# Final stage of a two-layer kernel: ScalarE normalizes seven of the eight pairs in one operation, VectorE multiplies by gamma and adds x in wide ones, GpSimd makes the biases

## What is computed

```
def _layer_norm(r, gamma, beta):
    mu = jnp.mean(r, axis=-1, keepdims=True)
    var = jnp.mean(jnp.square(r - mu), axis=-1, keepdims=True)
    return (r - mu) * jax.lax.rsqrt(var + LN_EPS) * gamma + beta
...
x = x + _layer_norm(z + out, gamma, beta)      # z = _layernorm(x)
```

## Time and profile before

| what | us |
|---|---|
| median of three runs | 1231.94 |
| profiled execution, its own time | 1231.25 |
| its span, first to last instruction | 1229.4 |
| last scatter into `dOUT` landed, first load of r issued | 1191.87 |
| last instruction of VectorE ends | 1224.96 |

### The profile page before, as it was taken

How to read it: one execution, slowest core, us unless ns; L and a number is a source line. 1 busy time by engine, 2 the same in 40 slices (tenths; PEclk the granted TensorE clock), 3 DMA queues, 4 the chain that set the end, 5 groups by cost and what they waited for, 6 DMA issues and landing times.

```text
span 1229.4 us, 24074 instructions
## 1 busy us (share of the span) xinstructions
PE 1095.7 (89%) x8282; PEld 1011.8 (82%) x8282; DVE 911.8 (74%) x1992; ACT 784.1 (64%) x1617; POOL 641.2 (52%) x573
## 2 busy tenths in 40 slices
PE   3678999988988999999999887999999999999950
PEld 2577887877876888888898777999999999999950
DVE  5787887686665666666657886899878778877868
ACT  4766666654234556555656666887778778877835
POOL 2444443442344556655644667886665544454435
PEclk8779999999899999999999988999999999999985
DMA  6644441231226579667746956556689766666539
GB/s 207 220 158 157 143 142 69 97 116 61 66 94 203 139 197 270 150 161 198 201 87 163 300 176 185 130 152 169 161 191 225 175 189 191 191 168 176 165 80 215
DMA packets 141864, 201.07 MB, mean 164 GB/s; under 512 B 28992, under 2 KB 115792, under 8 KB 134704
## 3 DMA queue, kind: packets, MB, share of 16 engines
q1 hardware_dynamic: 108880, 158.89, 39.0%
q0 software_dynamic: 32320, 40.13, 19.0%
q10 hardware_dynamic: 544, 0.52, 0.1%
HBM read 153.16 MB, written 46.48 MB: 162 GB/s over the span
## 4 chain that ended last, share of the span: by engine, by line
PE 70%; DVE 15%; DMA 4%; ACT 4%; issue 3%; POOL 2%; SPq 0%; DVEq 0%; ACTq 0%; POOLq 0%
PE pb L2198 16%; PE quad L2179 14%; PE quad L1230 13%; PE pb L1245 7%; PE pb L354 4%; PE quad L300 4%; PE pb L368 2%; DVE Dm L529 2%; PE quad L2173 2%; PE quad L2151 1%; PE pb L265 1%; PE pb L1214 1%; ACT Dm L841 1%; DMA x<-dACC 1%; DVE sm L1651 1%
## 5 line engine op out<-in xcount | busy, mean ns | idle before, releaser
L2411 POOL DMA_INDIRECT dOUT<-y,es x71 | 125.1, 1762 | 156.7 <-DVE y L2293 117.6
L2198 PE MATMUL pb<-wh,hh 128*128 128x256 f32 x568 | 163.7, 288 | 3.4 <-DVE hl L2280 3.4
L2198 PE MATMUL pb<-wh,hl 128*128 128x256 f32 x568 | 160.0, 282 | 0.0
L2198 PE MATMUL pb<-wl,hh 128*128 128x256 f32 x568 | 159.6, 281 | 0.0
L1404 POOL DMA_INDIRECT dACC<-ye,idxJ x64 | 100.3, 1567 | 97.4 <-ACT xeh L1343 46.5
L2365 ACT ACTIVATE gl<-quad,b1c 128x256 f32<-128x256 f32 (+1 forms) x312 | 124.2, 449 | 23.1 <-PE quad L2173 13.3
L2280 DVE TENSOR_TENSOR hl<-gl,hh 128x512 fp32r<-128x512 f32 (+1 forms) x156 | 98.7, 641 | 46.4 <-ACT hh L2373 46.1
L2198 PEld LDWEIGHTS pb<-wh,hh 128*128 128x128 f32 x568 | 108.1, 190 | 3.9 <-issue 2.6
L2198 PEld LDWEIGHTS pb<-wl,hh 128*128 128x128 f32 x568 | 107.4, 189 | 0.0
L2198 PEld LDWEIGHTS pb<-wh,hl 128*128 128x128 f32 x568 | 107.4, 189 | 0.0
L1357 ACT CAST ehh<-egf 128x512 fp32r<-128x512 f32 (+1 forms) x72 | 41.2, 572 | 101.8 <-DVE egf L1285 101.8
(11 more groups left out here) (336 smaller groups left out, 3334.1 us busy)
## 6 DMA issues: line engine op xcount, KB each, us to landing
w2r<-in_W SPq DMA_DIRECT2D x39, 1024.0 KB, 5.9
MB<-dM SPq DMA_DIRECT2D x16, 1024.0 KB, 5.3
wraw<-in_Wg SPq DMA_DIRECT2D x16, 512.0 KB, 6.7
wraw<-in_Wu SPq DMA_DIRECT2D x16, 512.0 KB, 8.1
wraw<-in_Wd SPq DMA_DIRECT2D x16, 512.0 KB, 5.4
W<-in_W SPq DMA_DIRECT2D x8, 1024.0 KB, 11.1
w1p<-in_W SPq DMA_DIRECT2D x7, 1024.0 KB, 7.8
b2c<-in_b SPq DMA_DIRECT2D x39, 128.0 KB, 3.0
```

Of the source, the lines that this page charges most:

```text
L2198: ins = pe.matmul(bank.t[:, 0:256], a_[s][:, c, 128 * tt:128 * tt + 128], b_[n % 3][:, 256 * c:256 * c + 256], start=half == 0 and m == 0, ...
L2411: g.indirect_dma_start(out=dOUT[:, :], out_offset=bass.IndirectOffsetOnAxis(ap=es[i % 6][:, tt, 1:2].bitcast(U32), axis=0), in_=y1[i % 2][ ...
```

## The change

ScalarE now computes (r - mean) * rstd itself for every pair but 5, as one activation a chunk with a scale and a bias per token (`normalized`). The bias is -mean * rstd, which GpSimd multiplies in a new small operation after each power (column 10). VectorE then multiplies the whole pair by gamma in one TENSOR_TENSOR of 1024 columns (`times_gamma`, into the new tile `gn`); for pairs 4, 6 and 7 it adds this to x in two of 512 (`plus_x`), and pairs 0 to 3 are accumulated from `gn`. Pair 5 keeps the old path. Pair 3's statistics go from ScalarE to VectorE, and `stats` gets one more small operation (minus the mean). The lists of calls are new, and SyncE stores in the order 4, 6, 7, 5.

```diff
-        BY_ACT = (1, 3, 5)
+        gn = M8.ring("gn", PAIRS, [128, 4, D])
+        BY_ACT = (1, 5)
+        SHIFTED = (5,)
...
                 v.wait_ge(*v_f.of("a", j))
+                v.tensor_scalar(s[:, :, 11:12], s[:, :, 6:7], -1.0, None, ALU.mult)
                 v.tensor_scalar(s[:, :, 9:10], s[:, :, 7:8], EPS, None, ALU.add).then_inc(*v_f.up("v", j))
...
+            def times_gamma(j):
+                v.wait_ge(*a_f.of("n", j))
+                v.tensor_tensor(gn[j][:, :, :], un[j][:, :, :], gam[:, :].unsqueeze(1).to_broadcast([128, 4, D]),
+                                ALU.mult).then_inc(*v_f.up("g", j))
+
+            def plus_x(j):
+                v.wait_ge(*v_f.of("g", j))
+                v.wait_ge(*v_f.of("beta", j))
+                for h in range(2):
+                    v.tensor_tensor(x2[j % 4][:, 2 * h:2 * h + 2, :], x2[j % 4][:, 2 * h:2 * h + 2, :], gn[j][:, 2 * h:2 * h + 2, :],
+                                    ALU.add).then_inc(*v_f.up("y", 2 * j + h))
...
             stats(0)
-            centre(0)
-            centre(1)
             stats(2)
+            times_gamma(0)
+            stats(3)
             variance(1)
-            centre(2)
-            centre(3)
             stats(4)
-            variance(3)
-            centre(4)
+            times_gamma(2)
             stats(6)
-            centre(6)
-            result(4)
+            times_gamma(3)
             stats(7)
-            result(6)
+            times_gamma(1)
             centre(5)
+            times_gamma(4)
+            plus_x(4)
             variance(5)
-            centre(7)
+            times_gamma(6)
+            plus_x(6)
+            times_gamma(7)
+            plus_x(7)
             result(5)
-            result(7)
...
+            def normalized(j):
+                if j not in BY_ACT:
+                    for b in (2 * j, 2 * j + 1):
+                        a.wait_ge(*fz_ld[b].of())
+                a.wait_ge(*g_f.of("bias", j))
                 for c in range(4):
-                    ins = a.activation(nc_[j][:, c, :], un[j][:, c, :], ACT.Copy, scale=fsm[j][:, c, 8:9])
-                    if c % 2:
-                        ins.then_inc(*a_f.up("n", 2 * j + c // 2))
+                    ins = a.activation(un[j][:, c, :], zc[j][:, c, :], ACT.Identity, scale=fsm[j][:, c, 8:9], bias=fsm[j][:, c, 10:11])
+                ins.then_inc(*a_f.up("n", j))
 
             sums(1)
+            normalized(0)
             squares(1)
-            scale(0)
-            sums(3)
-            squares(3)
-            scale(1)
-            scale(2)
-            scale(3)
+            normalized(2)
             sums(5)
+            normalized(3)
+            normalized(1)
             squares(5)
+            normalized(4)
+            normalized(6)
+            normalized(7)
...
+                if j not in SHIFTED:
+                    if j in BY_ACT:
+                        g.wait_ge(*a_f.of("m", j))
+                    g.wait_ge(*g_f.of("r", j))
+                    g.tensor_tensor(s[:, :, 10:11], s[:, :, 11:12], s[:, :, 8:9], ALU.mult).then_inc(*g_f.up("bias", j))
 
             def add(j):
+                g.wait_ge(*v_f.of("g", j))
                 for b in (2 * j, 2 * j + 1):
...
             power(0)
             power(2)
+            add(0)
+            power(3)
             power(1)
-            add(0)
             power(4)
-            power(3)
-            add(1)
             add(2)
             power(6)
+            power(7)
             add(3)
-            power(7)
             power(5)
+            add(1)
```

More of the change, by code:

```diff
@@ L2503, in build @@
         un = M8.ring("un", PAIRS, [128, 4, D])
-        nc_ = M8.ring("nc", ADDED, [128, 4, D])
-        BY_ACT = (1, 3, 5)
+        gn = M8.ring("gn", PAIRS, [128, 4, D])
+        BY_ACT = (1, 5)
+        SHIFTED = (5,)
         fz_ld = ring("moe_loaded", B)
@@ L2536, in centre @@
                 s = fsm[j]
[L2537 to L2545, removed]
+                v.wait_ge(*a_f.of("m", j))
+                for c in range(4):
+                    ins = v.scalar_tensor_tensor(out=un[j][:, c, :], in0=zc[j][:, c, :], scalar=s[:, c, 11:12], in1=gam[:, :],
+                                                 op0=ALU.add, op1=ALU.mult)
                 ins.then_inc(*v_f.up("u", j))
@@ L2563, in dve_stage5 @@
             stats(0)
-            centre(0)
-            centre(1)
             stats(2)
+            times_gamma(0)
+            stats(3)
             variance(1)
-            centre(2)
-            centre(3)
             stats(4)
-            variance(3)
-            centre(4)
+            times_gamma(2)
             stats(6)
-            centre(6)
-            result(4)
+            times_gamma(3)
             stats(7)
-            result(6)
+            times_gamma(1)
             centre(5)
+            times_gamma(4)
+            plus_x(4)
             variance(5)
-            centre(7)
+            times_gamma(6)
+            plus_x(6)
+            times_gamma(7)
+            plus_x(7)
             result(5)
-            result(7)
         def act_stage5(a):
             def sums(j):
-                if j > 1:
-                    a.wait_ge(*a_f.of("sum", j - 2))
+                if j == 5:
+                    a.wait_ge(*a_f.of("sum", 1))
                 for c in range(4):
@@ L2598, in squares @@
                 a.wait_ge(*a_f.of("m", j))
-                if j > 1:
-                    a.wait_ge(*a_f.of("squares", j - 2))
+                if j == 5:
+                    a.wait_ge(*a_f.of("squares", 1))
                 for c in range(4):
@@ L2603, in squares @@
                 ins.then_inc(*a_f.up("squares", j))
-            def scale(j):
-                a.wait_ge(*v_f.of("u", j))
-                a.wait_ge(*g_f.of("r", j))
+            def normalized(j):
[3 more added lines that the diff above has]
+                a.wait_ge(*g_f.of("bias", j))
                 for c in range(4):
-                    ins = a.activation(nc_[j][:, c, :], un[j][:, c, :], ACT.Copy, scale=fsm[j][:, c, 8:9])
-                    if c % 2:
-                        ins.then_inc(*a_f.up("n", 2 * j + c // 2))
+                    ins = a.activation(un[j][:, c, :], zc[j][:, c, :], ACT.Identity, scale=fsm[j][:, c, 8:9], bias=fsm[j][:, c, 10:11])
+                ins.then_inc(*a_f.up("n", j))
             sums(1)
+            normalized(0)
             squares(1)
-            scale(0)
-            sums(3)
-            squares(3)
-            scale(1)
-            scale(2)
-            scale(3)
+            normalized(2)
             sums(5)
+            normalized(3)
+            normalized(1)
             squares(5)
+            normalized(4)
+            normalized(6)
+            normalized(7)
         def pool_stage5(g):
@@ L2629, in power @@
                 g.tensor_tensor(s[:, :, 8:9], s[:, :, 9:10], mhalf[:, :].unsqueeze(1).to_broadcast([128, 4, 1]), ALU.pow).then_inc(*g_f.up("r", j))
+                if j not in SHIFTED:
[3 more added lines that the diff above has]
+                    g.tensor_tensor(s[:, :, 10:11], s[:, :, 11:12], s[:, :, 8:9], ALU.mult).then_inc(*g_f.up("bias", j))
             def add(j):
+                g.wait_ge(*v_f.of("g", j))
                 for b in (2 * j, 2 * j + 1):
-                    g.wait_ge(*a_f.of("n", b))
-                    g.dma_start(by_chunk(out[rows(b), :]), nc_[j][:, chunks(b), :], accum_op=ALU.add).then_inc(*out_ad[b].up(by=16))
+                    g.dma_start(by_chunk(out[rows(b), :]), gn[j][:, chunks(b), :], accum_op=ALU.add).then_inc(*out_ad[b].up(by=16))
             power(0)
             power(2)
+            add(0)
+            power(3)
             power(1)
-            add(0)
             power(4)
-            power(3)
-            add(1)
             add(2)
             power(6)
+            power(7)
             add(3)
-            power(7)
             power(5)
+            add(1)
         def sp_stage5(sp):
@@ L2653, in sp_stage5 @@
                 sp.dma_start(zc[b // 2][:, chunks(b), :], by_chunk(dOUT[of_tokens(rows(b)), :])).then_inc(*fz_ld[b].up(by=16))
-            for j in (4, 6, 5, 7):
+            for j in (4, 6, 7, 5):
                 for b in (2 * j, 2 * j + 1):
```

## The result

The changed kernel takes 1234.03 us, the kernel before 1230.65 (medians of 22 runs each); the ratio is 1.0028, with a 95% interval of 1.0017 to 1.0039. It is slower by 3.4 us (2.1 to 4.8).

What follows compares the result with a forecast made beforehand. VectorE and the DMA engines, ending within a microsecond of each other, were taken to bound the final stage; +1.4 us of DMA work and +0.6 us of GpSimd waits on 1231.94 gave 1233.9 us, range 1229.8 to 1237.6.

Steps and rivals of the forecast that it cites:

- VectorE alone would give 0.5 us: VectorE in the final stage: 1.9 us less work, with new waits, ends at 1224.5 against 1224.96.
- The product costs 0.45 us: GpSimd's new multiplication for the bias after each power, priced at 0.45 us, its wait for the power included.
- L2645 costs as much as L2640: Sign of a wrong forecast: GpSimd's product for the bias costs as much as a power, instead of 0.3 to 0.45 us.
- A wide operation beside GpSimd, 0.3 us for each of five operations behind 1212.5: Final stage: GpSimd's powers and products wait beside VectorE's wide operations; about 0.6 us at the end.
- the stage-1 row: Profile row: a small operation starting 0.05 us after a two-input SCALAR_TENSOR_TENSOR takes 0.51 us instead of 0.22.
- The hole of 2 us, and 12.0 us of DMA work behind it: DMA engines idle before pair 3's accumulations, then four accumulations and eight stores: end 1229.7 against 1228.3, +1.4 us.
- The end of the span: Behind VectorE's end: the last store lands 3.8 us after its start, and the span ends 0.6 us later.
- Rival 1: VectorE still ends the final stage, the DMA hole closes: 0.5 us less, 1231.4; chance 0.17.
- Rival 2: GpSimd's queue becomes the bound through dear products or waits for wide operations: +3.5 to +4.5 us, 1236; chance 0.20.
- Rival 3: DMA engines overlap accumulations and stores faster than counted, so the hole costs nothing: +0.4, 1232.3; chance 0.13.
- Rival 4: Stages 1 to 4 move though no instruction there changes; runs lie 4.1 us apart; chance 0.05.
- the last accumulation did start near 1222: Sign in the final stage: the last accumulation starts near 1222 and lands after the last store or with it.

Runs made afterwards that it cites:

- e3: The changed kernel without the accumulations of pair 1; stage 37.2 us, ratio to the kernel before 1.0006.
- e5: The changed kernel run again, unaltered; stage 41.3 us, ratio to the kernel before 1.0014.
- e1: The changed kernel without GpSimd's seven products for the bias; stage 39.7 us, ratio to the kernel before 1.0014.
- e2: The changed kernel with times_gamma as four operations of 256 columns instead of one of 1024; stage 39.8 us, ratio to the kernel before 1.0024.
- e4: The kernel before the change without the accumulations of pair 1; stage 35.6 us, ratio to the kernel before 0.9972.
- e8: The kernel before with accumulations issued as soon as their data are there, and variance(1) ahead of stats(2); stage 36.6 us, ratio 0.9985.
- e10: e8 run again, unaltered; stage 35.9 us, ratio to the kernel before 0.9978.
- e7: e2 with accumulations of pair 3 ahead of powers 6 and 7, and of pair 1 ahead of power 5; stage 38.8 us, ratio 0.9996.
- e9: e8 with the change's way for pair 7 only, its statistics, power and product moved ahead; stage 36.5 us, ratio to the kernel before 0.9996.

## Why the prediction held, and where it was mis-sized

The forecast was 2.0 us slower, 1233.9 us; measured are 3.4 us (2.1 to 4.8) and 1234.03. Direction, mechanism and range held, the size did not quite. That the time was met within 0.2 us is luck: the forecast was added to the median of three runs, 1231.94, which lies 1.3 us over the median of 22, and that made up for a step that was 1.4 us too small. In the traces the stage grew by 3.7 to 4.5 us. Point by point:

- **VectorE alone would give 0.5 us.** It gave nothing: its end went from 33.1 to 33.5 in one execution and 32.9 in the other. The terms: wait before `stats(2)` 2.4 instead of 1.9, before `times_gamma(0)` 0.24 instead of 0.6, and 0.28 before `times_gamma(3)`, where I had a cover of 0.5 us, which the late product of pair 3 used up.
- **The product costs 0.45 us.** Where it does not wait it takes 0.20, below my value. The price is in those that waited. "L2645 costs as much as L2640" was one of my signs of being wrong; at two places of seven it came true.
- **A wide operation beside GpSimd, 0.3 us for each of five operations behind 1212.5.** This is the term that was mis-sized, in its place above all. The products of pairs 3 and 4 waited 2.0 us in sum, ahead of the accumulations of pair 2, where I had put nothing. Of the five, the power of pair 6 ended 1.56 us after the generation ahead of it, where a power took 1.06 before, so it waited about 0.5; the power of pair 7 took 1.25, the two products 0.30 each, and the power of pair 5 did not wait: about 1 us instead of 1.5. The Trainium skill, SBUF — State Buffer, section Who interferes with whom, would let each wait for the whole of the wide operation, and at two places the trace agrees (1.28 and 1.16, each ending within 0.06 us of the operation beside it). I had set the stage-1 row (0.51) against the powers, which showed 0.1, and taken a mean. A mean over operations was the wrong tool for something that depends on where each starts.
- **The hole of 2 us, and 12.0 us of DMA work behind it.** Measured 1.5 and 11.9. The full work started 27.2 us into the stage, against 25.8 in my sum, and ended at 39.1, 2.7 us later than before, against 2.0 in my sum. The way of counting, work left over at the rates of the kernel before, is what carried the forecast. Its 3.6 accumulations left at 1217 were rough: the first two stores had been issued at 1214.2 and 1215.0, within the stretch that I counted as accumulations alone. e3 shows the backlog to be the cause; the hole is still in it.
- **The end of the span.** The last store landed 3.6 us later than before, 0.9 more than the full work ended later, and the span ended 0.9 later still. I had left both at what they were. Behind the landing 1.5 us pass where it was 0.6; in e5, e1 and e2 it is 1.8, 1.5 and 1.3, in e3, e4, e8 and e10 0.5 to 0.6. In every run with 0.9 or more, GpSimd's DRAIN ends at most 0.3 us before the span and behind the last landing. What the DRAIN waits for was not tried.
- **Rival 1 (VectorE still ends it)** is out by e3. **Rival 2 (GpSimd the bound)** is half true: its queue did slip by 2 us through wide operations, and its DRAIN ends the span, but VectorE did not wait for it at the end; most of the loss went over the DMA engines. **Rival 3 (overlap hides the hole)** is out: 11.9 us against 12.0. **Rival 4 (the rest of the kernel moves)** moved single executions, the four stages ahead by 3.4 us in the first pair; the 22 runs' 3.4 against the stage's 3.7 to 4.5 leaves it about 1 us at most.

Of my other signs, the last accumulation did start near 1222 (1218.2 in a stage that began 3.4 us earlier), but it landed 8.7 us later, 2.1 us before the last store and not with it.

## What to carry to other kernels

Where a stage's last stores land several microseconds after their issue, the chain's last engine isn't the bound alone: take the DMA work that was generated late out of it once (as e3 and e4 do) and see what the last landing does, before paying for a faster engine. Look behind the last landing too, for the engine whose DRAIN ends last. A small operation on GpSimd that reads SBUF took 0.2 to 0.5 us beside narrow VectorE operations here, once 1.64, and up to the whole of a wide one that it started in, so widening VectorE's operations can have a price on GpSimd's queue, and what is queued behind it there pays it. Accumulating DMAs, the dearest DMA work here, are best issued early, but e7 shows that what they delay on GpSimd counts as well.

## What the runs showed of the hardware

- In the changed kernel the waiting went one way only. GpSimd's products waited up to 1.1 us for VectorE, but every wide operation took 1.22 to 1.23 us, those that began while a power ran among them (a power from 1212.52 for 1.25 us, a TENSOR_TENSOR from 1212.85 for 1.23). A power that starts in the shadow of a wide operation waits too: in e9 one that starts 0.2 us into it takes 1.93 us.
- A power of four columns takes 1.00 to 1.26 us in these kernels where neither a DMA nor a wide VectorE operation is ahead of it, a product of the same shape 0.20 at its shortest: it is the function that costs, since the product's 0.20 holds the call as well.
- Of the DMA engines' full time an accumulation of 256 KB takes 1.97 us, 262 KB at 133 GB/s. At the end of the kernel before (1226.0 to 1227.0), with stores alone left, they move 382 GB/s, 0.69 us a store. The same bytes cost nearly three times as much when they are added.
- The span ends with the queue that closes last. GpSimd's DRAIN ended 1.3 us behind the last landing in the changed kernel and 0.4 behind it in the kernel before; in e3 it ended 0.3 us ahead of it, and the span ended 0.6 us after the landing.
